# Attention scores in four strips of 32 features, and the products for k and v moved to the front of each step

## The reference

```python
q = rms_norm(layernorm(x) @ w_q.T + b_q, g_q)          # 16 heads of 16 features
k = rms_norm(ctx @ w_k.T + b_k, g_k)
v = ctx @ w_v.T + b_v
s = einsum('bqhd,bkhd->bhqk', q, k) * SCALE            # within each batch entry of 64 tokens
x = x + softmax(s) @ v @ w_o.T + b_o
x = x + moe(layernorm(x))                              # top 4 of 32 experts, and a shared one
```

## Time and profile before

| | us |
|---|---|
| median of 3 runs | 858.23 (856.89 to 860.76) |
| the profiled execution, its time | 859.32 |
| its span, first to last instruction | 857.6 |
| PE busy | 774.5 (90% of the span) |
| DVE busy | 590.3 (69%) |
| POOL busy | 487.2 (57%) |
| ACT busy | 470.1 (55%) |

### The profile page before, as it was taken

How to read it: one execution, slowest core, us unless ns; L and a number is a source line. 1 busy time by engine, 2 the same in 40 slices (tenths; PEclk the granted TensorE clock), 3 DMA queues, 4 the chain that set the end, 5 groups by cost and what they waited for, 6 DMA issues and landing times.

```text
span 857.6 us, 22217 instructions
## 1 busy us (share of the span) xinstructions
PE 774.5 (90%) x6030; PEld 639.4 (75%) x6031; DVE 590.3 (69%) x2018; ACT 470.1 (55%) x1410; POOL 487.2 (57%) x692
## 2 busy tenths in 40 slices
PE   4899999999999999636999999999999999999995
PEld 2566666666666766415989989998998998988984
DVE  2578888888888888542656656665665665558886
ACT  2678888888888888313444444444444443332331
POOL 0126666666666666453655555555555556566775
PEclk9999999999999999857999999999999999999998
DMA  6345555555555556637634443443444342687775
GB/s 195 102 124 172 173 172 171 171 178 176 189 184 179 179 181 195 218 129 229 197 123 128 130 129 123 129 129 122 129 129 129 123 142 79 207 252 229 253 253 174
DMA packets 101890, 142.02 MB, mean 166 GB/s; under 512 B 16171, under 2 KB 83043, under 8 KB 101219
## 3 DMA queue, kind: packets, MB, share of 16 engines
q1 hardware_dynamic: 87523, 101.71, 40.3%
q0 software_dynamic: 14336, 39.94, 13.1%
HBM read 86.73 MB, written 58.82 MB: 170 GB/s over the span
## 4 chain that ended last, share of the span: by engine, by line
PE 41%; DMA 4%; issue 4%; DVE 2%; POOL 2%; SPq 1%; POOLq 0%; ACT 0%; DVEq 0%
PE bank L1196 9%; PE bank L1204 8%; PE bank L1218 6%; PE bank L1220 6%; PE bank L1211 4%; PE bank L1229 4%; DMA got<-yt_d 2%; DVE acc L1394 2%; DMA x2t<-xn2t_d 1%; PE bank L1267 1%; POOL scaled L1330 1%; PE bank L1247 1%; PE bank L1258 1%; PE bank L1254 1%; POOL part L1336 1%
## 5 line engine op out<-in xcount | busy, mean ns | idle before, releaser
L1319 POOL DMA_INDIRECT yt_d<-yo,name_i x160 | 157.9, 987 | 29.3 <-issue 20.3
L723 POOL DMA_INDIRECT xs_d<-rgu,sloti x128 | 128.5, 1004 | 41.6 <-issue 31.6
L1364 DVE TENSOR_TENSOR h<-bank,gated 128x176 f32<-128x176 f32 x160 | 54.6, 341 | 88.9 <-ACT gated L1282 88.9
L1196 PE MATMUL bank<-down_w,rdt 128*128 x320 | 97.6, 387 | 18.2 <-issue 17.1
L1204 PEld LDWEIGHTS bank<-ht,rd_w 88*128 88x128 f32 x640 | 96.5, 191 | 8.4 <-issue 0.4
L1278 ACT ACTIVATE rdt<-bank 128x128 f32<-128x128 f32 x160 | 44.3, 277 | 103.0 <-PE bank L1204 102.9
L1282 ACT ACTIVATE gated<-bank 128x176 f32<-128x176 f32 x160 | 50.7, 317 | 87.6 <-PE bank L1220 87.6
L1204 PE MATMUL bank<-ht,rd_w 88*128 88x128 f32 x640 | 97.6, 274 | 0.0
L1317 POOL TENSOR_TENSOR fence<-ones 128x1 f32<-128x1 f32 x160 | 29.5, 184 | 118.0 <-DVE name_i L1354 117.8
L1353 DVE COPY yo<-bank 128x256 f32<-128x256 f32 x160 | 67.2, 420 | 24.3 <-PE bank L1196 24.3
L1359 DVE COPY ht<-bank 88x256 f32<-88x256 f32 x160 | 67.3, 421 | 21.8 <-PE bank L1211 12.5
(11 more groups left out here) (163 smaller groups left out, 1933.4 us busy)
## 6 DMA issues: line engine op xcount, KB each, us to landing
xg<-xs_d SPq DMA_DIRECT2D x160, 128.5 KB, 2.1
got<-yt_d SPq DMA_DIRECT2D x32, 512.0 KB, 4.2
raw<-in_raw SPq DMA_DIRECT2D x32, 496.0 KB
v<-v SPq DMA_DIRECT2D x128, 34.0 KB, 2.1
xs_d<-in_spare SPq DMA_DIRECT2D x4, 1028.0 KB, 7.2
xin<-in_x SPq DMA_DIRECT2D x32, 128.0 KB
ctxt<-in_ctxt SPq DMA_DIRECT2D x32, 128.0 KB
xres<-in_x SPq DMA_DIRECT2D x32, 128.0 KB
```

The costliest lines, as they stand in the source:

```text
L723: nc.gpsimd.indirect_dma_start(xs_d, bass.IndirectOffsetOnAxis(sloti[:, b, k:k + 1], 0), rgu[:, b, k, :], None)\
L1196: nc.tensor.matmul(y_ps[b], rdt[:, b, :], weight(down_w, DOWN), start=True, stop=True)\
L1319: nc.gpsimd.indirect_dma_start(yt_d, bass.IndirectOffsetOnAxis(name_i[:, b, :], 0), yo[:, b, :], None)\
```

## The change

- Scores: `GROUPS, GH = 4, 2`: strips of 32 features, two heads each. The scores are 16 matmuls of 32 x 64 weights and 128 columns, into columns 0 to 255 of banks 0 to 3. k is copied with two masks and not four.
- PSUM: k and v (now a product each, four matmuls of 256 columns), the turn of q and the turn of k lie in columns 256 to 511 of banks 0, 1, 2 and 3.
- Order on PE: `kv_in` stands behind `x_turn`. It and `qk_turn` wait for the softmax's subtraction (`ssub_done`), `scores_ready` for the copies of k and v (`kb_done`, `v_done`). In step 3 the wait for the folded bias stands behind `qk_turn`.
- Order on ACT: the copy of v stands behind that of x. On DVE `k_bias` stands behind `gate_weights`, one step of DVE's earlier.

```diff
-GROUPS, GH = 2, 4
+GROUPS, GH = 4, 2
+STRIP = P // GROUPS
...
-            s_ps = bank03[:, 0:GROUPS, :]
-            kv_ps = bank03[:, 2, :]
-            qkt_ps = bank03[:, 3, :].rearrange("p (c t) -> p c t", c=2 * CH)
+            s_ps = bank03[:, 0:GROUPS, 0:DIM]
+            k_ps = bank03[:, 0, DIM:2 * DIM]
+            v_ps = bank03[:, 1, DIM:2 * DIM]
+            qt_ps = bank03[:, 2, DIM:2 * DIM].rearrange("p (c t) -> p c t", c=CH)
+            kt_ps = bank03[:, 3, DIM:2 * DIM].rearrange("p (c t) -> p c t", c=CH)
...
                     def kv_in(s, ph):
-                        if past(i, 1):
-                            pe.wait_ge(kb_done, i)
-                            pe.wait_ge(v_done, i)
+                        if past(i, 2):
+                            pe.wait_ge(ssub_done, i - 1)
                         pe.wait_ge(ld_ctx[b], landed(i, 2, b))
-                        for c in range(CH):
-                            m = nc.tensor.matmul(kv_ps, ctxt[:, b, c, :], wkv[:, c, :], start=(c == 0), stop=(c == CH - 1))
+                        for part, k in ((k_ps, 0), (v_ps, DIM)):
+                            for c in range(CH):
+                                m = nc.tensor.matmul(part, ctxt[:, b, c, :], wkv[:, c, k:k + DIM],
+                                                     start=(c == 0), stop=(c == CH - 1))
...
                     def qk_turn(s, ph):
+                        if past(i, 1):
+                            pe.wait_ge(ssub_done, i)
...
                     def scores_ready(s, ph):
                         pe.wait_ge(ktm_done, i + 1)
-                        if past(i, 1):
-                            pe.wait_ge(ssub_done, i)
+                        if live(i + 1, TILES):
+                            pe.wait_ge(kb_done, i + 2)
+                            pe.wait_ge(v_done, i + 2)
...
                                 for g in range(GROUPS):
-                                    feats = slice(64 * g, 64 * (g + 1))
-                                    m = nc.tensor.matmul(s_ps[SEQ * n:SEQ * (n + 1), g, c * 256:(c + 1) * 256],
+                                    feats = slice(STRIP * g, STRIP * (g + 1))
+                                    m = nc.tensor.matmul(s_ps[SEQ * n:SEQ * (n + 1), g, c * P:(c + 1) * P],
...
                     def body(s, ph):
                         if at_step(s, 1):
                             pe.wait_ge(ld_first, 16 * len(loads_first))
+                        x_turn(s, ph)
+                        kv_in(s, ph)
+                        down_product(s, ph)
+                        qk_turn(s, ph)
                         if at_step(s, 3):
                             pe.wait_ge(bo_done, 1)
                             pe.wait_ge(halves_done, 2)
-                        x_turn(s, ph)
-                        down_product(s, ph)
-                        qk_turn(s, ph)
                         p_turn(s, ph, 0)
                         q_in(s, ph)
                         p_turn(s, ph, 1)
-                        kv_in(s, ph)
                         scores_ready(s, ph)
```

More of the change, by code:

```diff
@@ L426, in p_times_v @@
                         for blk in range(PAIRS):
-                            group, c, hp = blk // 4, blk // 2 % 2, blk % 2
-                            pair = PAIRS // CH * c + GH // 2 * group + hp
+                            group, c = blk // CH, blk % CH
+                            pair = PAIRS // CH * c + group
                             for n in range(2):
@@ L633, in body @@
                             nc.scalar.activation(xn1t[:, b, :, :], xnt_ps, ACT.Copy).then_inc(xnt_done, 1)
+                            act.wait_ge(kv_psum, i + 1)
+                            if past(i, 2):
+                                act.wait_ge(v2_in[b], landed(i, 2, b, 64) - 64)
+                            nc.scalar.activation(
+                                v17[:, b, :, :, 0:HD],
+                                v_ps.rearrange("p (r g d) -> p r g d", r=2, g=PAIRS),
+                                ACT.Copy).then_inc(v_done, 1)
                         e = s - 1
@@ L640, in body @@
                             for c in range(CH):
-                                nc.scalar.activation(qt[:, b, c, :], qkt_ps[:, c, :], ACT.Copy,
+                                nc.scalar.activation(qt[:, b, c, :], qt_ps[:, c, :], ACT.Copy,
                                                      scale=gqk[:, c:c + 1])
@@ L671, in body @@
                                                  accum_out=ssq[:, b, 1:2]).then_inc(ssq_done, 1)
-                            if past(i, 2):
-                                act.wait_ge(v2_in[b], landed(i, 2, b, 64) - 64)
-                            nc.scalar.activation(
-                                v17[:, b, :, :, 0:HD],
-                                kv_ps[:, DIM:2 * DIM].rearrange("p (r g d) -> p r g d", r=2, g=PAIRS),
-                                ACT.Copy).then_inc(v_done, 1)
                         i, b = s - 5, (ph - 5) % 2
@@ L831, in soft @@
                             return
-                        sv = s_ps.rearrange("p g (h k) -> p (g h) k", k=SEQ)
-                        mv = smax[:, b, :, :].rearrange("p g h -> p (g h)")
                         dve.wait_ge(smax_done, i + 1)
                         nc.vector.tensor_tensor(
-                            prob[:, b, :, :].rearrange("p q (r k) -> p (q r) k", r=2), sv,
-                            mv.unsqueeze(2).broadcast_to([P, HEADS, SEQ]), ALU.subtract).then_inc(ssub_done, 1)
+                            prob[:, b, :, :].rearrange("p (g c) (r k) -> p g (c r) k", c=CH, r=2),
+                            s_ps.rearrange("p g (h k) -> p g h k", k=SEQ),
+                            smax[:, b, :, :].unsqueeze(3).broadcast_to([P, GROUPS, CH * GH, SEQ]),
+                            ALU.subtract).then_inc(ssub_done, 1)
                     def q_bias(s, ph):
@@ L846, in k_bias @@
                     def k_bias(s, ph):
-                        i, b = s - 1, (ph - 1) % 2
+                        i, b = s, ph % 2
                         if not live(i, TILES):
                             return
-                        if at_step(s, 1):
+                        if at_step(s, 0):
                             dve.wait_ge(ld_next, 16 * len(loads_next))
                         dve.wait_ge(kv_psum, i + 1)
-                        nc.vector.tensor_tensor(kb[:, b, :], kv_ps[:, 0:DIM], bk[:, :], ALU.add).then_inc(kb_done, 1)
+                        nc.vector.tensor_tensor(kb[:, b, :], k_ps, bk[:, :], ALU.add).then_inc(kb_done, 1)
                     def o_norm(s, ph):
@@ L981, in body @@
                         norm1_mean(s, ph)
-                        k_bias(s, ph)
                         soft_max(s, ph)
@@ L994, in body @@
                         gate_weights(s, ph)
+                        k_bias(s, ph)
                         norm2(s, ph)
```

11 lines of the change are left out of this document (5 added, 6 removed).

## The result

The changed kernel takes 877.62 us in the median of four runs (874.9 to 880.79), the kernel before, timed beside it, 858.88 (856.89 to 860.76). The ratio is 1.0226, with a 95% interval of 1.0197 to 1.0254: slower by 18.7 us, where 27.2 were forecast. The profiled execution took 874.90 us, with a span of 873.2 (857.6 before).

What follows compares the result with a forecast made beforehand. PE was taken to pace the attention stage, with ACT and DVE close behind. 29 steps of 1.04 us more (30.2), less 3 at the ends, made 27.2 more: 885.4 us forecast, range 870 to 901.

Steps and rivals of the forecast that it cites:

- the halved copies of k give nothing: On ACT before `x2_turn`: two copies of k instead of four save nothing, since the second half of the probabilities comes late anyway.
- The size of the wait: PE in front of `x2_turn`: stands some 1.3 us for ACT's `down_w`, so `x2_turn` starts 1.27 us later each step.
- The scores: From `scores` to the product with v: 0.80 us instead of 1.03, saving 0.23; bounds 0.43 less and 0.03 more.
- The sum: Attention stage: 29 steps each 1.04 us longer make 30.2, less 3 at the ends, so 27.2 us more.
- my own case: Whole kernel: slower through PE's wait for `down_w`, 885.4 us, bounds 876.6 and 895.9; chance 0.83.
- The ends: Start and drain of the attention stage: together about 3 us come back, bounds 0 and 6.
- the 2.22 in step 3: PE's wait for the folded bias in front of `x_turn` in step 3: all 2.22 us taken to come back.
- the 0.71 for k in the drain: First step of the drain: the 0.97 us wait for k shrinks by two copies, 0.71 us.
- ACT held the stage: Rival, attention stage: ACT paces the step and gets relief, 23.6 us less, 834.6 us; chance 0.05.
- the two balance: Rival, each step: the wait before `x2_turn` about equals the scores' saving, 858 us, give or take 4; chance 0.04.
- the eight pieces might not work side by side: Rival, scores: streams run one behind another, scores take 3.52 us, 109 more in all, 964 us; chance 0.03.
- The falling clock: Rival, each step: the new wait drops TensorE's clock to 1.2 GHz for 4 us, 85 more, 943 us; chance 0.05.

Runs made afterwards that it cites:

- e1_down_early: The changed kernel, with ACT's copy of `down_w` moved from behind the second half of the probabilities to behind the copy of v: 853.68 us.
- e2_move_alone: The kernel before, with only the move of k and v behind `x_turn`, v's copy and `k_bias` moved too; old strips, banks, four k copies: 927.95 us.
- e5_before_down_early: The kernel before, with ACT's copy of `down_w` moved in front of the copies of q: 857.72 us.

## Why the prediction was right

**The bound and the mechanism.** `kv_in` was ACT's cover, and without it `x2_turn` waits for `down_w`: forecast with that releaser, found in every step, and proved by e1_down_early, which takes the wait away and gets 24 us. e2_move_alone shows that the move alone is slower. One sentence of the working was wrong without harm to the sum: that the halved copies of k give nothing. By its own figures four copies would have kept ACT until 5.63 and not 5.14, and with four, in e2_move_alone, `x2_turn` starts 0.67 later.

**The size of the wait.** Forecast 1.27 us later for `x2_turn`, measured 1.13 (5.97 less 4.84). The walk, the step as I laid it out, ended 0.14 too late (6.11 and 5.97). The largest term in this is `kv_in`, at 1.85 us, where eight records take 1.73 (202.80 to 204.53). I had taken 1.82 from two starts with no wait named between them and added 0.03, but 0.10 of that distance was already the wait for `down_w` (e5_before_down_early). ACT's copy of `down_w` also took 0.38 where I had 0.44, and its copy of the second half followed PE's by 0.03 and not 0.11; against these, `x2_turn` came 0.14 and not 0.05 behind `down_w`, and ACT's start on q 0.70 and not 0.64 behind `qk_turn`. That these nearly cancel is luck. On DVE `k_bias` filled the gap in front of the second norm as laid out: that norm starts 3.27 after `x_turn` (3.34 before).

**The scores.** Forecast 0.80 (0.60 to 1.06), measured 0.63. The nearer row was the scores' own and not the product with v. At 208.92 and 209.10, 0.05 and 0.23 behind the group's start at 208.87, the records in flight were:

```profile
L506 PE MATMUL bank<-ktm,qt x8: 318/318/319, 208.9 to 208.9; 32*64 32x128 f32 x8
...
L506 PE MATMUL bank<-ktm,qt x16: 267/293/319, 208.9 to 209.1; 32*64 32x128 f32 x16
```

Eight within the first 0.05 us and sixteen by 0.23: rounds of eight, one for each piece of the array, 0.16 us apart, where 4 x (0.11 + 0.04) was the lower bound's working. In the same kernel the product with v, with as many records, still takes 1.05 (209.50 to 210.55 in the trace). Its 33 ns a record are therefore no pace at which PE issues. The floor of about 25 ns between starts that the Trainium skill names ("TensorE: Matmul & The Clock Gate", section "Wait — 56ns, not 53.3ns?") would have made 0.80; 32 records in 0.63 us are 20 ns each, and the measurement decides against it for records on different pieces of the array. In steps: 0.40 saved and not 0.23.

**The sum.** 29 x 1.04 was forecast, with bounds of 0.84 and 1.30 a step; the mean step grew by 0.69, and the typical one by 0.76, of which 1.13 - 0.40 = 0.73 are the two terms above. Both fall under the lower bound, since both terms were off in the change's favour. With 29 x 0.69 = 20.0, less 2.8 at the start and 0.9 in the drain, the same sum gives 16.3 for the two traces, whose spans differ by 15.6; the medians differ by 18.7. The measured 877.6 us is just above the 876.6 that I had as the lowest of my own case, so the time lies well inside the stated range by its added margin. The ends came out as a sum (3.7 against 3) and not by the terms: of the 2.22 in step 3 only 0.58 of waiting went, and the rest of the 2.8 is time gained before step 3 and a clock that no longer fell; of the 0.71 for k in the drain 0.15 came, since the second norm holds `x2_turn` there.

**The rivals.** That ACT held the stage was wrong as put, but e5_before_down_early shows a true part in it: PE looked full in the earlier trace rows, and yet waited 0.10 us for ACT, and with that gone it waited for DVE in every other step. That the two balance did not come: the wait of 1.05 is far over the 0.40 saved, and the second half of the probabilities did wait for the first. That the eight pieces might not work side by side is refuted by the 0.63. The falling clock did not come, though e2_move_alone shows how near it was.

## What to carry to other kernels

A long matmul between two others may be there for another engine's sake: before it is moved, count what that engine does meanwhile and put its copies into the order in which PE now asks for them. When one engine's wait goes, look at once for the engine that is next: in the changed kernel ACT's order gave 24 us, and behind it POOL's order 5 and the place of PE's own wait 6, while the first of these alone gave nothing in the kernel before. A distance between two starts is a duration only if the second had nothing to wait for, even where the trace names no wait.

## What the runs showed of the hardware

- Thirty-two float32 records with weights of 32 x 64 and 128 columns, on eight pieces of the array, take 0.63 us; sixteen with 64 x 64 and 256 columns, on four, took 1.03. The product with v, 32 records of 128 x 64 and 34 columns on two pieces, takes 1.05.
- The clock fell to 0.50 behind a wait of 1.66 us, the only one that the timeline names in the step, but in eight of 28 such steps only (and in part in a ninth), and cost about 3.1 us each time (15.1 in place of 12.0). It also fell behind the wait of 2.22 us in step 3 of the kernel before. With waits of 1.05 us in a step of 11 it never fell between steps 4 and 32. What decides between the steps in which it falls and the others was not tried.
- ACT's copy of `down_w` (128 x 256) took 437 ns in the mean before and 378 after. That PE waits beside it is not the reason: in e2_move_alone PE waits too and the copy takes 438, in e1_down_early it does not and the copy takes 385. The cause stays open.
- The name that a trace puts to a wait can be that of the wrong one of two: in the drain it is k's, whose copies had ended 0.80 us before PE went on; the second norm had ended 0.10 before.
